# A sequence layer on one core: VectorE also sums the probabilities of the first short chunk, and the last norm's steps change places

## The reference, cut to what matters

```
paths = sigmoid(x @ Wp + bp)                     # 8 heads, 5 numbers per token and head
agree = pq * pk + (1 - pq) * (1 - pk)
sim   = cumprod(agree, -1).sum(-1) / 5           # causal: -inf above the diagonal
attn  = softmax(sim)
ctx   = attn @ (x @ Wv)                          # per head, head width 32
x     = layernorm(x + ctx @ Wo)
gate, up = x @ wg.T, x @ wu.T                    # int weights / 127, hidden width 768
x     = layernorm(x + (silu(gate) * up) @ wd.T)
```

## Time and profile before

| what | value |
|---|---|
| median of three runs | 829.33 us |
| profiled execution, its own time | 829.72 us |
| its span | 828.0 us |
| TensorE busy | 786.7 us, 95% |
| VectorE busy | 609.6 us, 74% |
| ScalarE busy | 453.8 us, 55% |
| GpSimd busy | 292.3 us, 35% |
| mean granted TensorE clock | 0.989 |
| ones matmuls of `probs` into `den_ps` (L938) | 82.5 us busy |

### The profile page before, as it was taken

One profiled execution on the slowest core, in us unless ns is written; L12 is line 12 of the kernel. 1 busy time (PEld: TensorE's weight loads), 2 busy tenths in 40 slices (PEclk: granted clock), 3 DMA queues, 4 the chain that ended last, 5 costly groups with the idle time before them and its releaser, 6 DMA issues.

```text
span 828.0 us, 14242 instructions
## 1 busy us (share of the span) xinstructions
PE 786.7 (95%) x5442; PEld 381.5 (46%) x5442; DVE 609.6 (74%) x1081; ACT 453.8 (55%) x705; POOL 292.3 (35%) x266
## 2 busy tenths in 40 slices
PE   6998999999999999999999999999999999799976
PEld 5452364443644445443644436444554435244343
DVE  2768876699667976789666996679767897558667
ACT  1655645667365655657456673656556574365422
POOL 0202342336224262244423362242622444134324
PEclk9999999999999999999999999999999999899999
DMA  7842555044720826125540437207260255301011
GB/s 226 198 126 77 127 138 144 1 95 95 194 77 1 179 74 157 50 51 129 142 139 1 108 83 193 77 1 179 77 153 1 52 127 139 91 1 27 26 26 53
DMA packets 81301, 79.39 MB, mean 96 GB/s; under 512 B 37712, under 2 KB 60496, under 8 KB 81232
## 3 DMA queue, kind: packets, MB, share of 16 engines
q1 hardware_dynamic: 81232, 78.46, 37.8%
HBM read 53.28 MB, written 16.78 MB: 85 GB/s over the span
## 4 chain that ended last, share of the span: by engine, by line
PE 56%; DVE 23%; issue 9%; ACT 5%; DMA 3%; SPq 1%; POOL 1%; DVEq 0%; POOLq 0%; ACTq 0%
PE slot L909 9%; PE ctx_ps L932 9%; PE misc L969 9%; PE misc L982 7%; PE misc L883 7%; PE misc L955 6%; DVE acc L629 6%; PE den_ps L938 5%; DVE work L730 4%; ACT probs L531 4%; DVE x L712 4%; DVE acc L626 3%; DVE work L738 1%; DMA xT_sb<-in_xT_dram 1%; SPq L381 1%
## 5 line engine op out<-in xcount | busy, mean ns | idle before, releaser
L531 ACT ACTIVATE probs<-slot 128x1024 f32<-128x1024 f32 (+3 forms) x384 | 290.2, 808 | 256.0 <-PE slot L909 236.5
L460 POOL TENSOR_SCALAR_AFFINE_SELECT probs<-probs 128x512 f32<-128x512 f32 x128 | 143.2, 1119 | 210.1 <-ACT probs L531 210.0
L474 POOL TENSOR_TENSOR work<-work 128x512 f16<-128x512 f32 x96 | 116.8, 1217 | 163.6 <-ACT work L551 163.6
L932 PE MATMUL ctx_ps<-probs,vz_sb 128*32 128x512 f32 (+3 forms) x1536 | 164.7, 501 | 2.6 <-DVE ctx_raw L639 2.6
L909 PE MATMUL slot<-query_stack,key_stack 128*128 128x512 f16 (+3 forms) x768 | 160.0, 329 | 4.5 <-ACT probs L531 3.9
L969 PE MATMUL misc<-x1T_hi,w_parts 128*128 128x512 f16 x358 | 138.5, 387 | 9.3 <-DVE phi_lo L606 3.8
L969 PE MATMUL misc<-x1T_lo,w_parts 128*128 128x512 f16 x358 | 138.2, 386 | 0.0
L909 PEld LDWEIGHTS slot<-query_stack,key_stack 128*128 128x128 f16 x768 | 56.3, 98 | 164.1 <-issue 119.3
L730 DVE SCALAR_TENSOR_TENSOR work<-work,misc 128x512 f32<-128x512 f32 x90 | 61.5, 683 | 66.3 <-ACT work L545 65.5
L629 DVE TENSOR_TENSOR acc<-acc,probs 128x1536 f32<-128x1536 f32 (+3 forms) x60 | 95.0, 1584 | 0.6 <-POOL probs L460 0.5
L938 PE MATMUL den_ps<-probs,ones 128*32 128x512 f32 (+3 forms) x800 | 82.5, 484 | 0.0
(11 more groups left out here) (75 smaller groups left out, 707.6 us busy)
## 6 DMA issues: line engine op xcount, KB each, us to landing
key_stack<-phi_dram SPq DMA_DIRECT2D x56, 256.0 KB, 5.8
query_stack<-phi_dram SPq DMA_DIRECT2D x56, 256.0 KB, 6.3
x_sb<-in_x_dram SPq DMA_DIRECT2D x8, 1024.0 KB, 5.4
out_dram<-x SPq DMA_DIRECT2D x15, 512.0 KB, 4.1
xT_sb<-in_xT_dram SPq DMA_DIRECT2D x7, 1024.0 KB, 5.0
phi_dram<-phi_hi SPq DMA_DIRECT2D x14, 256.0 KB, 2.0
phi_dram<-phi_lo SPq DMA_DIRECT2D x14, 256.0 KB, 2.3
key_stack<-phi_dram SPq DMA_DIRECT2D x16, 128.0 KB, 3.1
```

The lines of the kernel that those rows point to most:

```text
L460: pool.affine_select(out=tile, in_=tile, compare_op=ALU.is_ge, fill=0.0, base=0, pattern=[[0, 4], [1, P]], channel_multiplier=-1).then_inc ...
L474: pool.tensor_tensor(hid_lo[:, n % M1, :], hid[:, n % HSLOTS, :], hid_hi[:, n % M1, :], ALU.subtract).then_inc(hid_lo_ready, 1)
L531: act.activation(probs[:, s % P_SLOTS, 2 * p:2 * p + 2, off:CH], slot[p][:, :, off:CH], ACT.Exp).then_inc(slot_drained[p], 1)
L932: mm = pe.matmul(ctx_ps[32 * k:32 * k + 32, off:CH], vz_sb[:, b % 2, j, 32 * h:32 * h + 32], probs[:, s % P_SLOTS, k, off:CH], start=first ...
```

## The change

For batches 1 to 7, block 0 now also goes through `acc`: its four tiles are added by VectorE in three sums, the first of which copies the 128 columns that the second tile lacks. TensorE's four ones matmuls of block 0 become one group over `acc`, as in blocks 2 and 3, now with `start=True`. In slots 1 to 4 the order is rewritten: the statistics of the last norm of batch b-1's first half move from slot 1 to slot 2, behind block 3's `normalise`; their `apply` and the store move from slot 2 to the middle of slot 3's projection; the sums stand at the ends of slots 2 and 3 and in slot 4 behind `bias`. Batch 0 keeps its plan.

```
-    ADD_FROM = {2: 3, 3: 1}
+    ADD_FROM = {0: 0, 2: 3, 3: 1}
...
     def added(b, i):
-        return i in ADDED and i <= SUM_END[b, STEPS[i][0]]
-    NA = len(ADD_FROM)
+        q, c, g, j = STEPS[i]
+        return i in ADDED and not (b == 0 and c == 0) and not (b == B - 1 and q == NQ - 1 and i in DIAG)
...
-        1: down(-1, 0, 1) + norm(1, -1, 0),
-        2: vz(1, 0, 1) + [("apply", 1, -1, 0), ("store", -1, 0)],
-        3: project(-1, 1) + norm(0, -1, 1),
-        4: vz(1, 2, 3, 4) + [("load_x", 0), ("apply", 0, -1, 1), ("bias", 1, 0)] + turn_x1(-1, 1) + [("squash", 1, 0)],
+        1: down(-1, 0, 1),
+        2: vz(1, 0, 1) + norm(1, -1, 0) + [("sum", 0, 1)],
+        3: (project(-1, 1)[:2] + [("apply", 1, -1, 0), ("store", -1, 0)] + project(-1, 1)[2:] + norm(0, -1, 1)
+            + [("sum", 0, 2)]),
+        4: (vz(1, 2, 3, 4) + [("load_x", 0), ("apply", 0, -1, 1), ("bias", 1, 0), ("sum", 0, 3)] + turn_x1(-1, 1)
+            + [("squash", 1, 0)]),
...
                 if j == ADD_FROM[q] + 1:
...
-                    dve.tensor_tensor(acc[:, :, :], probs[:, (s - 1) % P_SLOTS, :, :], own, ALU.add).then_inc(summed, 1)
+                    first = probs[:, (s - 1) % P_SLOTS, :, :]
+                    if off:
+                        dve.tensor_copy(acc[:, :, 0:off], first[:, :, 0:off])
+                    dve.tensor_tensor(acc[:, :, off:CH], first[:, :, off:CH], own, ALU.add).then_inc(summed, 1)
...
                 if added(b, i) and i == SUM_END[b, q]:
-                    pe.wait_ge(summed, len(ADDS) * b + ADDS.index(i) + 1)
+                    pe.wait_ge(summed, SUMS[b, i] + 1)
+                    alone = ADD_FROM[q] == 0
+                    if alone and NQ * b + q >= 1:
+                        pe.wait_ge(den_out, NQ * b + q)
                     for k in range(4):
-                        mm = pe.matmul(den_ps[32 * k:32 * k + 32, :], ones[:, :], acc[:, k, :], start=False, stop=final)
+                        mm = pe.matmul(den_ps[32 * k:32 * k + 32, :], ones[:, :], acc[:, k, :], start=alone, stop=final)
```

More of the change, by code:

```diff
@@ L46, in seq_postln_kernel @@
     DIAG = [i for i, (q, c, g, j) in enumerate(STEPS) if j >= TC * c]
-    ADD_FROM = {2: 3, 3: 1}
+    ADD_FROM = {0: 0, 2: 3, 3: 1}
     ADDED = [i for i, (q, c, g, j) in enumerate(STEPS) if q in ADD_FROM and j >= ADD_FROM[q]]
     ADDS = [i for i in ADDED if STEPS[i][3] > ADD_FROM[STEPS[i][0]]]
-    SUM_END = {(b, q): max(i for i in ADDED if STEPS[i][0] == q and not (b == B - 1 and q == NQ - 1 and i in DIAG))
-               for b in range(B) for q in ADD_FROM}
     def added(b, i):
-        return i in ADDED and i <= SUM_END[b, STEPS[i][0]]
-    NA = len(ADD_FROM)
+        q, c, g, j = STEPS[i]
+        return i in ADDED and not (b == 0 and c == 0) and not (b == B - 1 and q == NQ - 1 and i in DIAG)
+    SUM_END = {(b, q): max(i for i in ADDED if STEPS[i][0] == q and added(b, i))
+               for b in range(B) for q in ADD_FROM if any(STEPS[i][0] == q and added(b, i) for i in ADDED)}
+    SUMS = {at: n for n, at in enumerate((b, i) for b in range(B) for i in ADDS if added(b, i))}
+    SUMMED = {at: n for n, at in enumerate(SUM_END)}
     LAST = {q: max(i for i, s in enumerate(STEPS) if s[0] == q) for q in range(NQ)}
@@ L144, in between @@
             n[at] += b
+            if what == "sum" and tuple(n) not in SUMS:
+                continue
             if 0 <= n[at] < B and (what not in ("load_x", "load_xT", "stack") or n[at] > 0):
@@ L180, in attention @@
                 plan += [("mask", b, i)]
-        if s >= 1 and (s - 1) % NS in ADDS and added(*divmod(s - 1, NS)):
-            plan += [("sum", *divmod(s - 1, NS))]
-        plan += between(b, i)
+        sums = [("sum", *divmod(s - 1, NS))] if s >= 1 and divmod(s - 1, NS) in SUMS else []
+        plan += between(b, i) if STEPS[(s - 1) % NS][1] == 0 else sums + between(b, i)
         if LAG <= s < B * NS - 1:
@@ L527, in exps @@
                         i2 += i2 not in ADDS
-                        act.wait_ge(summed, len(ADDS) * b2 + ADDS.index(i2) + 1)
+                        act.wait_ge(summed, SUMS[b2, i2] + 1)
                 for p in range(2):
@@ L615, in add_up @@
                 own = probs[:, s % P_SLOTS, :, off:CH]
-                count = len(ADDS) * b + ADDS.index(i)
+                count = SUMS[b, i]
                 if i in DIAG:
@@ L622, in add_up @@
                 if j == ADD_FROM[q] + 1:
-                    used = NA * b + list(ADD_FROM).index(q)
-                    if used:
-                        dve.wait_ge(acc_used, used)
-                    dve.tensor_tensor(acc[:, :, :], probs[:, (s - 1) % P_SLOTS, :, :], own, ALU.add).then_inc(summed, 1)
+                    if SUMMED[b, q]:
+                        dve.wait_ge(acc_used, SUMMED[b, q])
+                    first = probs[:, (s - 1) % P_SLOTS, :, :]
+                    if off:
+                        dve.tensor_copy(acc[:, :, 0:off], first[:, :, 0:off])
+                    dve.tensor_tensor(acc[:, :, off:CH], first[:, :, off:CH], own, ALU.add).then_inc(summed, 1)
                 else:
@@ L634, in normalise @@
                 dve.wait_ge(pv_done, NS * b + LAST[q] + 1)
-                if q in ADD_FROM:
-                    dve.wait_ge(acc_used, NA * b + list(ADD_FROM).index(q) + 1)
+                if (b, q) in SUMMED:
+                    dve.wait_ge(acc_used, SUMMED[b, q] + 1)
                 if Q >= 1:
```

## The result

The changed kernel took 841.40 us (median of 4 runs, 840.21 to 844.82), the kernel before 829.86 in the same comparison. The ratio is 1.0152, with a 95% interval of 1.0123 to 1.0181: slower, as forecast, by 11.5 us between the medians where 13.7 were forecast. The profiled execution is the slowest of the four: 844.82 us, span 843.1, that is 15.1 over the span before.

The account below looks back on a forecast made before the run. Bound: the x1T_lo DMA ahead of slot 6's gate, reached through VectorE. Steps 0.61, first rsqrt 0.43 and second 0.91 put x1_hi 1.96 us late; seven batches, 13.7 us, make 843.4 from 829.72 (843.0 from the median); range 831.5 to 848.

Parts of the forecast that it names:

- The bound: Slot 6's first gate matmul: follows the x1T_lo DMA's landing, 3.1 us after issue, reached through VectorE, not TensorE's work.
- What TensorE saves: Block 0's ones groups, four replaced by one over acc: 1.63 us a batch, 11.4 in seven, if all reached the end.
- The steps on VectorE: Slots 1 to 4, normalise to second apply: without any conflict, x1_hi starts 0.61 us late.
- The conflict on the second rsqrt: GpSimd's rsqrt beside the 256 wide sum: statistics to second apply 4.05 us in place of 3.14, 0.91 more.
- The conflict on the first rsqrt: GpSimd's rsqrt between copy and first sum: delays that sum by 0 to 0.88 us, taken as 0.43.
- the mask's case: Earlier GpSimd mask beside a VectorE sum: held back all but 0.13 us, then made x1_lo 0.43 us longer.
- the lock that the prediction cites: VectorE and GpSimd share SBUF ports exclusively, first comer keeping them; literally, the first rsqrt would cost nearly 0.88 us.
- What hides the rest: Block 0's ones group: TensorE waits up to 2.6 us for acc, yet beats the later DMA, so no own cost.
- The clock: Rival: TensorE's waits bring the 1.2 GHz level in six more batches, 12 us more, 855 us; chance 0.06.
- The rival that would be faster: TensorE's 11.4 us count, giving 818, if VectorE's stretch to the second apply is under 12.6 us; chance 0.05.

Follow-up runs that it names:

- Ones kept: Changed kernel with all VectorE sums, but TensorE again multiplies block 0's tiles by ones and ignores those sums: 840.42 us, 1.0135 to the kernel before.
- the last pair of runs: Changed kernel with the last norm's statistics in slot 5, apply and store in slot 7; with block 0's sums 817.21 us, without them 825.76 us.
- the other: Second profiled execution of the changed kernel, without an edit: 838.53 us, span 836.8 us.
- The last version: Changed kernel with the last norm's statistics in slot 5, apply and store in slot 7, block 0's sums kept: 817.21 us, 0.9854 to the kernel before.
- block 1 runs: Block 1 instead of block 0 through acc, against the changed kernel: 830.13 us with the old order of slots 1 to 4, 828.39 us with the new.
- sum 2 behind apply: Changed kernel with the 256 wide sum moved from ahead of the second apply to behind it: 837.73 us, 1.0095 to the kernel before.

## Why the prediction was right, step by step

*The bound.* Right, and shown: the gate starts 3.1 to 3.3 us behind the issue of x1T_lo in every run, in batches 1 to 7, where the value matmuls ran at the full clock and the landing was an ordinary one. Ones kept shows that TensorE's saving did not count, the last pair of runs that it counts once the way to `x1_hi` is shorter too.

*What TensorE saves.* Too high, though the forecast did not rest on it: 1.63 forecast, 1.26 measured. In the last pair of runs slot 6's value matmuls start 419.40 - 402.06 = 17.34 us behind block 3's ones group with the sums, and 423.03 - 404.43 = 18.60 without them. What the sum left out: without a ones group behind them the matmuls into `ctx_ps` take longer to the next start, in slot 2 of batch 4 1.00 us where it was 0.88, and about as much more in slots 3 and 4.

*The steps on VectorE.* Copy 0.34 (417.69 to 418.03), first sum 1.68 for 1.66, first `apply` 1.69, statistics to second `apply` 4.04 for 4.05: as worked out. The second `apply` ended after 1.68 instead of 1.77.

*The conflict on the second rsqrt.* Right in size: 0.91 forecast, 1.92 - 1.01 measured. Its length follows the sum beside it: 1.92 us beside 1024 elements, 1.39 beside 512, 1.01 beside none.

*The conflict on the first rsqrt.* Wrong: 0.43 forecast, nothing measured. The rsqrt lost 0.11 to the copy, and the sum behind it ran 1.75, as the 1.74 of the earlier trace rows, while the rsqrt was still recorded. Taking the mask's case for it was the mis-sized term; it makes 3 us of the forecast's 13.7. By the lock that the prediction cites from the Trainium skill (SBUF — State Buffer, section "SBUF: two separate sides"), taken literally, it would have cost twice that; the measurement decides against both. Why this sum and the rsqrt did not hold each other stays open.

*What hides the rest.* Right at full clock: TensorE waited for `acc` (1.51 where up to 2.6 were reckoned: the group started 0.6 us earlier behind block 3's ones group than worked out, and TensorE reached it 0.5 us later) and still reached the gate 0.5 us ahead of the DMA. At the low clock it was not: the value matmuls took 1.5 us more and the gate followed them, not the landing.

*The clock.* I gave it 0.06 as a matter of every batch, at 2 us each. It came in some batches, at 0.95: five of six in one execution, one of six in the other. That the waits are split did not prevent it. `x1_hi` 1.36 us late in batch 1, 1.43 in five and 1.84 in the last makes 10.4; five low stretches of 0.95 bring that to the 15.1 of the profiled execution. How many of them the unprofiled runs had can't be read, so how much of the measured 11.5 is the clock stays open; ones kept, with none in batches 1 to 6 of its profiled execution, lost 11.1 between its medians. What decides whether the clock falls stays open too.

*The rival that would be faster.* Its condition was stated as VectorE's stretch under 13.9 us for a gain of 0.36 a batch. The last version has 415.94 - 403.10 = 12.84 and gained 1.39; the rule would give 1.42.

## What to carry to other kernels

An engine that reads 99% busy is the bound only where nothing else ends at the same moment: look for the instruction at which a DMA lands together with it, and follow that DMA back before crediting a saving. What work costs on an engine with idle time depends on what it stands ahead of there: nothing was lost in the block 1 runs, though the saving was used up by another chain, and 1.4 us a batch where VectorE feeds the critical transfer. The cure here was to move other work out of that stretch into single gaps, and both halves (less on TensorE, less on VectorE) were needed. An order of two engines' instructions that start together on the same memory is worth a look in the trace: here a 1 us helper doubled.

## What the runs showed of the hardware

An rsqrt of 4 elements on GpSimd (1.01 us alone) that started 0.17 to 0.18 us behind a VectorE instruction on `probs` and `acc` ended 0.86 to 0.88 us after that instruction's end in every batch, whether it was a sum of 1024 elements, a sum of 512 or a copy of 512. A sum of 1536 that started 0.16 us behind the rsqrt was not held back by it: 1.75 us beside it, and 1.75 in the last version with no rsqrt near. The low granted clock came behind waits of TensorE of 1.4 to 1.5, 0.1 and 0.3 us in 6 of 12 such batches, with no difference ahead of it that the profile shows; a single wait of 1.7 us at that place, in six batches of sum 2 behind apply, did not bring it. The transposing DMA ahead of the gate landed after 3.0 to 3.2 us in batches 1 to 7 of every run, but after 4.4 in batch 4 of both block 1 runs and 4.0 in batch 5 of sum 2 behind apply.
